# A graph network on one core: which queue issues the second layer's loads during the first layer's messages

## The reference

```python
h = jnp.maximum(_layernorm(x, axis=-1), 0.0)
x = x + _L0_gnn_ref(h, node_vec1, edge_attr_16, edge_attr_4, src, dst, ...)
h = jnp.maximum(_layernorm(x, axis=-1), 0.0)
x = x + _L1_gnn_ref(h, edge_attr_3, edge_attr_64, ..., edge_index)
```

## Time and profile before

| | us |
|---|---|
| timed runs | 9671.8, 9685.46, 9688.35 |
| median of the timed runs | 9685.46 |
| span of the profiled execution | 12324.9 |
| first messages in that span (line 1445's first gather to 7900) | 2838 to 7900 |
| GpSimd busy in the span | 7006.2 (57%) |
| DVE / PE / ACT busy in the span | 7264.9 / 7174.4 / 4965.0 |

### The profile page before, as it was taken

The page is one execution under the profiler, slowest core; times in us unless marked ns, Lnnn a source line. Parts: engine busy times, 40 slices in busy tenths (PEclk is TensorE's granted clock), DMA queues, the critical chain, the costliest instruction groups (busy, mean ns, idle before and its releaser), DMA issues. The chain is left out here.

```text
span 12324.9 us, 170670 instructions
## 1 busy us (share of the span) xinstructions
PE 7174.4 (58%) x31166; PEld 4913.0 (40%) x31166; DVE 7264.9 (59%) x21188; ACT 4965.0 (40%) x16490; POOL 7006.2 (57%) x7069
## 2 busy tenths in 40 slices
PE   4444444444545545455555555577677777777778
PEld 3222222222222222222222222255566777677668
DVE  6444444444555555555655555566566666676665
ACT  2333333333333333333333333333455555555554
POOL 3555555556666666666665666555555555555551
PEclk7555555556777777777777777778788888888889
DMA  2222222223333333333333334444444444444457
GB/s 80 72 71 71 73 72 72 71 72 107 108 111 109 111 108 110 108 108 111 111 109 106 112 108 110 99 136 136 117 119 121 121 119 118 121 121 121 119 116 185
DMA packets 826473, 1315.62 MB, mean 107 GB/s; under 512 B 228520, under 2 KB 627624, under 8 KB 826280
## 3 DMA queue, kind: packets, MB, share of 16 engines
q0 software_dynamic: 337920, 667.48, 19.7%
q1 hardware_dynamic: 417496, 547.30, 14.7%
q10 hardware_dynamic: 70992, 100.14, 2.3%
HBM read 862.45 MB, written 914.08 MB: 144 GB/s over the span
## 5 line engine op out<-in xcount | busy, mean ns | idle before, releaser
L1445 POOL DMA_INDIRECT feat_m<-feat_tab,rows_m x3712 | 3704.0, 998 | 2622.5 <-issue 1195.9
L1545 PE MATMUL pair<-prod_m,hot_m 128*128 128x160 f32 x14848 | 2479.6, 331 | 906.1 <-DVE prod_m L1751 845.7
L1545 PEld LDWEIGHTS pair<-prod_m,hot_m 128*128 128x128 f32 x14848 | 2360.3, 215 | 1025.3 <-issue 830.8
L1522 PE MATMUL bank<-prod_m,hot_m 128*128 128x449 f32 x2476 | 1409.4, 703 | 1964.1 <-DVE prod_m L1788 1191.8
L1578 ACT ACTIVATE prod_m<-part_m,rows_m 128x64 f32<-128x64 f32 x5568 | 1431.4, 337 | 2783.0 <-issue 1347.7
L1566 ACT ACTIVATE hot_m<-hot_m,rows_m 128x128 f32<-128x128 f32 x5568 | 1728.6, 389 | 1675.9 <-DVE hot_m L1734 1345.5
L1809 DVE SCALAR_TENSOR_TENSOR acc_m<-acc_m,same_block,pair 128x640 f32<-128x640 f32 (+1 forms) x1237 | 1025.1, 829 | 2191.9 <-remote 1673.8
L652 POOL DMA_INDIRECT sorted_rows<-rows_e,place_e x1664 | 1602.4, 963 | 1124.5 <-ACT place_e L687 622.4
L1464 POOL DMA_INDIRECT sorted_rows<-later_m,place_m x1248 | 1281.1, 1027 | 848.3 <-ACT place_m L1626 496.6
L1522 PEld LDWEIGHTS bank<-prod_m,hot_m 128*128 128x128 f32 x2476 | 537.0, 238 | 2777.2 <-issue 2682.6
L478 PE MATMUL pair<-fc,hT_e 64*128 64x192 f32 x3328 | 632.9, 544 | 1277.6 <-ACT rows_e L681 1240.6
(11 more groups left out here) (250 smaller groups left out, 9521.6 us busy)
## 6 DMA issues: line engine op xcount, KB each, us to landing
agg_tab<-acc_m ACTq DMA_DIRECT2D x928, 320.0 KB
rows_m<-sorted_rows SPq DMA_DIRECT2D x928, 229.0 KB
agg_tab<-acc_m ACTq DMA_DIRECT2D x928, 224.5 KB
rows_m<-sorted_rows SPq DMA_DIRECT2D x928, 197.0 KB
feat_m<-feat_tab,rows_m POOLq DMA_INDIRECT x3712
turned_m<-in_turned ACTq DMA_DIRECT2D x159, 256.0 KB
agg_s<-agg_tab SPq DMA_DIRECT2D x98, 320.0 KB, 3.6
sorted_rows<-rows_e,place_e POOLq DMA_INDIRECT x1664
```

The source lines that it names most:

```text
L1445: pool.indirect_dma_start(out=feat[s % RING][:, k, :], out_offset=None, in_=g.feat_tab[l.n], in_offset=bass.IndirectOffsetOnAxis(ap=rows[s ...
L1522: mm = pe.matmul(out[:, 0, :], hot[s % l.hot_bufs][:, k, 0, :], prod[s % prods][:, k, 0:l.agg], start=(k == 0), stop=(k == ST_TILES - 1))
L1545: mm = pe.matmul(dst, hot[s % l.hot_bufs][:, k, q, :], rhs, start=(k == 0 and col == 0), stop=(k == ST_TILES - 1), skip_group_check=True)
```

## The change

In the first messages the loads of second-layer attributes and small fields are issued by SP in place of ACT. SP loads the first two chunks' data and the third chunk's attributes ahead of its first group of rows; in the turns it issues a pair of loads behind the group at step 4 (from the second turn on) and behind the group at step 8, each load behind a wait of its own. ACT keeps the Relu and the stores of sums. The four waits for the last loads at the end go from ACT to SP. What is loaded, into which buffers, is as before.

```diff
-            turns(sp, STEPS, TURN, group, upto=NST // TURN)
+            def load_turned(c, h):
+                sp.dma_start(turned[h][:, :], ...).then_inc(turned_here[h], 16)
+
+            def load_meta(c, h):
+                sp.dma_start(meta[h][:, :, :], ...).then_inc(meta_here[h], 16)
+
+            def attributes(c, h):
+                sp.wait_ge(hid_ready, c + 2)
+                load_turned(c + 3, 1 - h)
+                sp.wait_ge(copied, c + 1)
+                load_meta(c + 2, h)
+
+            def step_(step, it, s):
+                group(step, it, s)
+                if sends and s == 4 and (step is None or step >= TURN):
+                    attributes(it * PER_TURN - 1, 1)
+                if sends and s == 8:
+                    attributes(it * PER_TURN, 0)
+            if sends:
+                for c in range(2):
+                    load_turned(c, c)
+                    load_meta(c, c)
+                sp.wait_ge(hid_ready, 1)
+                load_turned(2, 0)
+            turns(sp, STEPS, TURN, step_, upto=NST // TURN)
+            if sends:
+                attributes(NCHUNK0 - 1, 1)
+                for h in range(2):
+                    sp.wait_ge(turned_here[h], 16 * (NCHUNK0 // 2 + 2 - h))
+                    sp.wait_ge(meta_here[h], 16 * (NCHUNK0 // 2 + 1))
...
             def hidden_act(c, h):
                 act.wait_ge(hid_ready, c + 1)
-                load_turned(c + 2, h)
                 act.activation(hT[h][:, :], hid[:, :], ACT.Relu).then_inc(hT_ready, 1)
...
-                w = window(step, it, s, 5)
-                if w is not None:
-                    c, h, n, known = w
-                    act.wait_ge(copied, c + 1)
-                    load_meta(c + 2, h)
...
             if sends:
-                for c in range(2):
-                    load_turned(c, c)
-                    load_meta(c, c)
                 hidden_act(0, 0)
```

More of the change, by code:

```diff
@@ L1433, in group @@
                                      "(p k) w -> p (k w)", k=ST_TILES), WIDE_LANES)).then_inc(rows_here[slot], 16)
-            turns(sp, STEPS, TURN, group, upto=NST // TURN)
+            def load_turned(c, h):
+                sp.dma_start(turned[h][:, :],
+                             lanes(t["turned1"][bass.ds(c * 2 * L1.fc_in, 2 * L1.fc_in), :], WIDE_LANES)
+                             ).then_inc(turned_here[h], 16)
+            def load_meta(c, h):
+                sp.dma_start(meta[h][:, :, :],
+                             lanes(t["meta1"][bass.ds(c * P, P), :], SMALL_LANES)).then_inc(meta_here[h], 16)
+            def attributes(c, h):
[21 more added lines that the diff above has]
+                    sp.wait_ge(meta_here[h], 16 * (NCHUNK0 // 2 + 1))
         @block.gpsimd
@@ L1580, in outer @@
                 ins.then_inc(outer_ready, 1)
[L1582 to L1585, removed]
             def hidden_act(c, h):
                 act.wait_ge(hid_ready, c + 1)
-                load_turned(c + 2, h)
                 act.activation(hT[h][:, :], hid[:, :], ACT.Relu).then_inc(hT_ready, 1)
-            def load_meta(c, h):
-                act.dma_start(meta[h][:, :, :],
-                              lanes(t["meta1"][bass.ds(c * P, P), :], SMALL_LANES)).then_inc(meta_here[h], 16)
             def prepare(step, it, s):
@@ L1662, in _ @@
                 act.wait_ge(acc_stored[s], 16 * ((NST - s + l.accs - 1) // l.accs))
[L1663 to L1666, removed]
         @block.vector
```

## The result

The changed kernel takes 9706.2 us (median), the kernel before 9684.0 in the same comparison: a ratio of 1.0025, with a 95% interval of 1.0018 to 1.0032. It is slower by about 22 us where I had forecast +6.9. The time lies inside the range of 9590 to 9740, but 1 us past the 9705 above which I had called the forecast wrong, and on the side to which I had given 0.16.

A forecast was written before the change was run, and what follows sets the result against it. GpSimd's pace of issuing indirect DMAs was taken to bound the first messages; 0 + 0 + 0 + 6.85 gave +6.9 us on 9685.46, so 9692.3, own range 9670 to 9704, stated range 9590 to 9740.

The forecast's parts named there:

- GpSimd's pace bounds the kernel: First messages, timed run: 20 indirect DMAs a chunk of about 0.98 + 0.30 us set the time, some 25.6 us.
- The recording is no copy of a timed run: Whole kernel: 2639.4 us of the 12324.9 us span exist only under the profiler; 7.1% of GpSimd's waits live on.
- the slow stretches live on in timed runs: First messages: ACT's stalls behind its loads are real and leave with them; 9620, at most down to 9490; chance 0.20.
- the profile holds at face value: First messages: all 1011.5 us of GpSimd's named waits are real and could go, 8681; chance 0.03.
- the stretches go to SP: First messages: stalls follow the loads to SP and delay row groups; 234 us in half the chunks, 9926; chance 0.12.
- signs of a right forecast: Changed kernel's trace: ACT's idle time without a wait far below 1347.7 us, GpSimd's waits for places below 496.6 us.
- ACT relieved of 347 us: First messages: ACT loses the issuing of 317 loads, which lay beside its own arithmetic; effect nothing.
- SP takes 317 loads: First messages: SP issues them at 1.27 us a chunk, 2.19 at most, within its parked time; effect nothing.
- SP's new waits delay no rows: Turns of the first messages: everything SP waits for is done before the next row group could go out; cost nothing.
- The start: 6.85 us: Stage's start: SP's loads and wait ahead of its first rows delay the first gather by 6.85 us, bounds 0 to 7.4.
- slower shifts of GpSimd's pace: Leftover case: GpSimd's own pace becomes slower for other reasons; no size given, chance 0.04.
- a mild part of SP's slow stretches: First messages: a weaker form of stalls moving to SP, taken in by the range's room up to 9740.

The follow-up runs named there:

- turns on SP: Against the kernel before: the turns' loads issued by SP, the five loads at the stage's start left on ACT; ratio 1.0017.
- quiet on SP: Against the kernel before: turns' loads on SP, meant for ACT's old moments, though one load still went out behind a row group; ratio 1.0007.
- the second recording of the same kernel: The unchanged kernel before, run and recorded once more; span 9673.9 us for an execution of 9675.7, ratio 1.0004.
- the runs without the start: Against the kernel before, start's loads on ACT: all turns' loads on SP behind row groups, 1.0017; only the attributes there, 1.0020.
- Late on ACT: Against the kernel before: all loads stay on ACT, but the turns' loads are issued later, right behind SP's row loads; ratios 1.0000 and 1.0007.

## Why the prediction was right and wrong

**GpSimd's pace bounds the kernel.** Right. From its first gather to its last indirect DMA the stage is GpSimd's busy time plus 945 to 957 us of idle time in all thirteen clean recordings, and the 0.30 us between its 3104 DMAs make up nearly all of that. Where its gathers grow by 16 us (1837.7 - 1821.9, turns on SP) the runs grow by 16 (ratio 1.0017). Single recordings follow the runs only roughly: quiet on SP has 21 us more of gathers and a ratio of 1.0007.

**The recording is no copy of a timed run.** Right, and shown: the second recording of the same kernel has 9673.9 us. With it fall the rivals that the slow stretches live on in timed runs (9620), that the profile holds at face value (8681) and that the stretches go to SP (9926): there were none to be won or moved. The rule of the Trainium skill, Runtime: NRT & Kernel Launch (preamble and postamble), of a constant 6.2 us between profile and runtime is closer for the clean recordings, though the run is longer than the span there, by 1.8 us (9675.7 and 9673.9); the span counts from first to last instruction and need not be the total that the page means. What I had named as signs of a right forecast, ACT's idle time and the places' waits falling, was no test: both fall in the unchanged kernel too.

**ACT relieved of 347 us: nothing.** Right. With the turns' loads off ACT and at nearly the same times on SP the ratio is 1.0004.

**SP takes 317 loads: nothing for the issuing.** Right: 0.616 us a load of attributes, and SP is parked for 2730.5 us.

**SP's new waits delay no rows.** Right but for one stretch: of 30.5 us of waits for rows in the stage 17.6 are the first gather's and 7.4 three waits near 6150 and 6206 us, the rest the 0.30 us between two DMAs. In the second recording no wait for rows behind the first gather is longer than 0.3 us; whether the loads have to do with that one stretch is not shown.

**The start: 6.85 us.** Right in mechanism and size, 6.4 to 6.95 measured.

**The step that failed** is the end of the same paragraph on SP's waits. I worked out that the loads would go out at steps 12t-1 and 12t+4, found that their own users need them some 30 us later, and wrote "Cost nothing". I had priced the issue and the user, and not the transfer: 256 KB right behind 788 KB of rows, with the gather of step 11 in flight. Nothing in that paragraph asks which other transfer lands at that time. The missing term, put at nothing there, is some 15 us: what the start leaves of the 22, and 16 and 19 us in the runs without the start (1.0017, 1.0020). The trace showed the question, if not the price: before, ACT's load goes out at 7013.90, in a gap between row groups (and row loads at 7006.09 in the earlier trace rows). The 0.04 that I had left for slower shifts of GpSimd's pace is where the result lies. That the time lies inside the range is luck: the room above 9705 was kept for a mild part of SP's slow stretches, and these did not come.

On the queue itself the Trainium skill, DMA: Bandwidth & Descriptors (Issuing engines are not separate DMA queues), says that DMAs of all issuers run on the same sixteen engines and interleave, so that another issuer saves the sequencer's time and no more. The runs agree as far as SP goes: at nearly ACT's times 1.0004. Late on ACT does not fit, with some 3 us where attributes behind the rows cost 16 to 19 on SP.

## What to carry to other kernels

Moving a load to another queue moves its transfer in time: beside the issue's price and the user's slack, list which transfers are in flight at the new moment and who waits for those. If a recording's span is far from the runs, record the unchanged kernel again before reading any stall out of it. On a kernel bound by indirect DMAs of GpSimd, sum their durations by place in the loop: here a shift of VectorE by a microsecond changed them without a wait in the profile.

## What the runs showed of the hardware

The length of an indirect DMA on GpSimd depends on where VectorE stands. Of the gathers beside which VectorE ran no instruction at all (220 to 331 in each of the thirteen recordings, worked out from their rows) none took over 0.99 us, and the mean was 0.96. Beside VectorE's instructions the same gather of step 2 takes mostly 0.95, 1.02 or 1.53 us, by where it meets VectorE's products. The Trainium skill, GPSIMD Engine Reference (Specifications), says that GpSimd shares its SBUF interfaces with VectorE and contends with VectorE's instructions that read two SBUF inputs or run in a 2-port mode. The three products are of the first kind, and the trace fits: all 117 long gathers start 0.10 to 0.14 us behind the first of them. But a plain share of VectorE's time is not what counts: 153 us more of reduces, which read one input, gave a ratio of 0.9996.

The same load costs SP about half of ACT's issuing time, 0.616 us against 1.13 (medians; the earlier trace rows, and the same in the second recording), which was worth nothing here.
